# Padding rows written behind each expert's last row instead of a cleared row store, and another order of the first attention group

## What is computed

```python
x = x + attn(layernorm(x), w_qkv, w_proj, q_gain)
    # 16 query heads, 4 key/value heads of size 16, RMS norm and rotary embedding of q and k, causal softmax
x = x + ffn(layernorm(x), ...)
    # scores = sigmoid(x @ w_router); each token goes to its best 2 of 8 experts with normalised weights
    # expert: silu(x @ w1[e]) * (x @ w3[e]) @ w2[e], hidden width 176
    # plus a shared expert of hidden width 352 for all tokens
```

## Time and profile before

| | us |
|---|---|
| median of 3 runs | 584.66 (582.53 to 585.18) |
| profiled execution | 584.15 |
| its span | 582.2 |
| TensorE busy | 474.1 (81%) |
| ScalarE busy | 362.3 (62%) |
| VectorE busy | 313.5 (54%) |
| GpSimd busy | 170.9 (29%) |

### The profile page before, as it was taken

One profiled execution on the slowest core, in us unless ns is written; L12 is line 12 of the kernel. 1 busy time (PEld: TensorE's weight loads), 2 busy tenths in 40 slices (PEclk: granted clock), 3 DMA queues, 4 the chain that ended last, 5 costly groups with the idle time before them and its releaser, 6 DMA issues.

```text
span 582.2 us, 9830 instructions
## 1 busy us (share of the span) xinstructions
PE 474.1 (81%) x3202; PEld 264.9 (45%) x3202; DVE 313.5 (54%) x886; ACT 362.3 (62%) x567; POOL 170.9 (29%) x222
## 2 busy tenths in 40 slices
PE   1694869999999999999398768859797889999930
PEld 1582323233333333333143424327675789998920
DVE  6973516834713156131276555535957567666726
ACT  4255759989999989998369556615242335555520
POOL 3721101011110220103241172044455824444430
PEclk9878969999999999999599987868899989999985
DMA  8111012963999469243521022211011434444349
GB/s 207 31 48 41 11 32 86 301 163 98 289 296 282 112 48 4 1 92 98 145 55 57 2 74 86 62 43 56 28 57 40 124 74 119 124 117 125 110 138 340
DMA packets 77525, 61.36 MB, mean 105 GB/s; under 512 B 26984, under 2 KB 70600, under 8 KB 77480
## 3 DMA queue, kind: packets, MB, share of 16 engines
q1 hardware_dynamic: 73784, 51.04, 36.7%
q0 software_dynamic: 3408, 9.34, 4.5%
q10 hardware_dynamic: 288, 0.39, 0.2%
HBM read 19.88 MB, written 29.34 MB: 85 GB/s over the span
## 4 chain that ended last, share of the span: by engine, by line
PE 48%; DVE 18%; issue 14%; DMA 5%; POOL 5%; ACT 5%; SPq 4%; another core or an unknown queue 1%; DVEq 0%; ACTq 0%; POOLq 0%
PE ps L1575 16%; PE ps L1555 10%; PE ps L1747 6%; ACT prob L783 4%; PE ps L1765 3%; POOL rows_by_expert L658 2%; SPq L369 2%; PE ps L1584 2%; PE ps L1495 2%; DVE sm L922 2%; DMA yfin<-pair_out 2%; DVE sm L921 2%; PE ps L1769 1%; POOL hid_lo L687 1%; PE ps L1516 1%
## 5 line engine op out<-in xcount | busy, mean ns | idle before, releaser
L783 ACT ACTIVATE prob<-ps 128x1024 f32<-128x1024 f32 (+3 forms) x320 | 260.1, 919 | 70.6 <-PE ps L1555 68.6
L1575 PE MATMUL ps<-prob,v_sb 128*32 128x512 f32 (+3 forms) x1280 | 158.3, 569 | 18.3 <-DVE o_sb L1073 9.6
L1555 PE MATMUL ps<-qk 64*128 64x512 f32 (+3 forms) x640 | 121.1, 442 | 20.4 <-DMA qk<-qT 12.3
L617 POOL TENSOR_SCALAR_AFFINE_SELECT prob<-prob 128x512 f32<-128x512 f32 x64 | 41.3, 647 | 228.3 <-ACT prob L783 227.3
L1555 PEld LDWEIGHTS ps<-qk 64*128 64x128 f32 x640 | 54.1, 192 | 114.5 <-ACT prob L783 82.2
L1575 PEld LDWEIGHTS ps<-prob,v_sb 128*32 128x32 f32 x1280 | 26.0, 110 | 64.7 <-issue 34.0
L719 POOL DMA_INDIRECT pair_out<-yo,xg x39 | 37.5, 963 | 54.7 <-DVE yo L1431 54.4
L1073 DVE COPY o_sb<-ps 128x512 f32<-128x512 f32 x16 | 11.1, 691 | 65.2 <-PE ps L1575 64.6
L1693 PE MATMUL ps<-x2T,ws_hi 128*128 128x512 f32 (+1 forms) x96 | 33.0, 427 | 4.4 <-DVE hid L1300 4.4
L658 POOL DMA_INDIRECT rows_by_expert<-xs,slots x32 | 31.4, 981 | 14.2 <-issue 8.7
L1060 DVE CAST qT<-ps 96x512 fp32r<-96x512 f32 x16 | 11.0, 686 | 36.8 <-PE ps L1516 36.8
(11 more groups left out here) (203 smaller groups left out, 782.0 us busy)
## 6 DMA issues: line engine op xcount, KB each, us to landing
rows_by_expert<-pads SPq DMA_DIRECT2D x9, 1935.0 KB, 19.8
qk<-qT SPq DMA_DIRECT2D x138, 64.0 KB, 2.1
xg<-rows_by_expert SPq DMA_DIRECT2D x39, 129.0 KB
yfin<-pair_out SPq DMA_DIRECT2D x8, 512.0 KB, 7.3
stage<-in_w SPq DMA_DIRECT2D x8, 352.0 KB
x_sb<-in_x SPq DMA_DIRECT2D x4, 512.0 KB, 7.3
qk<-shT SPq DMA_DIRECT2D x8, 256.0 KB, 4.8
res<-in_x SPq DMA_DIRECT2D x4, 512.0 KB, 4.2
```

The source lines that it names most:

```text
L617: nc.gpsimd.affine_select(out=t, in_=t, compare_op=ALU.is_ge, fill=0.0, base=0, pattern=[[0, HPG], [1, P]], channel_multiplier=-1).then_in ...
L783: nc.scalar.activation(prob[:, u % NPB, 2 * hf:2 * hf + 2, c0:CH], ps[:, b:b + 2, c0:CH], ACT.Exp, scale=SCALE).then_inc(exp_done, 1)
L1555: ins = M(ps[:, 2 * (n % NSB) + h, c0:CH], qk[rows, par, PAIRS, kt * P:(kt + 1) * P], qk[rows, par, hf, j * CH + c0:(j + 1) * CH], start=T ...
L1575: ins = M(ps[VW * h:VW * (h + 1), O_BANK, c0:CH], v_sb[:, kt, :], prob[:, u % NPB, h, c0:CH], start=(kt == 0), stop=(u == LAST_OF[j]), ski ...
```

## The change

It does two things.

Rows: rows_by_expert is no longer filled. Each segment is T + 128 rows long (SEG). A new DRAM tensor `pad_rows` has 15 blocks of 128 padding rows (zeros with row numbers), one block to each of the 8 experts and to each of the 7 spare tiles. One DMA writes the zeros behind the moves of group 0, one the numbers behind those of group 1, and one copies the 7 spare blocks into place behind those of group 2. When the last `place` is done, VectorE casts `reach` to integers (`ends`). SyncE, behind its last weight load, waits for that and copies one block behind each expert's last row: 8 times a register load and a DMA from DRAM to DRAM. It then waits for all padding and all scattered rows before the gathers. `pair_out` shrinks. GpSimd's wait before the first scatter is removed.

First group: the round of chunk 1 stands ahead of `attend`, the round of chunk 2 at step 7 instead of 8, that of chunk 3 at step 14 instead of 16, and the output of chunk 0 at step 8 instead of 4. The scores of units 4 and 5, the first of chunk 1, are issued behind the value product of unit 3. VectorE's order follows.

```diff
-ROWS = E * T + SPARE * P
-PADS = 15
+SEG = T + P
+ROWS = E * SEG + SPARE * P
+PADS = E + SPARE
 FIRST_GROUP = {
-    0: [("round", 0, 1)], 4: [("out", 0, 0)], 8: [("round", 0, 2)], 12: [("out", 0, 1)], 16: [("round", 0, 3)],
+    7: [("round", 0, 2)], 8: [("out", 0, 0)], 12: [("out", 0, 1)], 14: [("round", 0, 3)],
...
+        pads_d = nc.dram_tensor("pad_rows", (PADS * P, ROW), F32, kind="Internal").ap()
+        pair_d = nc.dram_tensor("pair_out", (2 * T + PADS * P, D), F32, kind="Internal").ap()
...
             sp.wait_ge(consts, CONSTS)
-            clear_rows(0, 3)
+            sp.dma_start(pads_d.rearrange("(k p) c -> p k c", p=P), pads[:].broadcast_to([P, PADS, ROW])).then_inc(zeroed, 16)
             for c in range(NC):
                 move(1, c)
-            sp.wait_ge(s_ready, 2 * NU)
-            clear_rows(3, blocks)
+            sp.wait_ge(zeroed, 16)
+            sp.dma_start(pads_d[:, ID:ID + 1].rearrange("(k p) c -> p k c", p=P), pad_ids[:].bitcast(F32),
+                         allow_slow_non_contiguous=True).then_inc(padded, 16)
             for c in range(NC):
                 move(2, c)
-            sp.wait_ge(zeroed, 16 * blocks)
-            for b in range(blocks):
-                sp.dma_start(rows_d[b * PADS * P:(b + 1) * PADS * P, ID:ID + 1].rearrange("(k p) c -> p k c", p=P),
-                             pad_ids[:, b * PADS:(b + 1) * PADS, :].bitcast(F32),
-                             allow_slow_non_contiguous=True).then_inc(padded, 16)
+            sp.wait_ge(padded, 16)
+            sp.dma_start(rows_d[E * SEG:ROWS, :], pads_d[E * P:PADS * P, :]).then_inc(padded, 16)
             for c in range(NC):
                 move(3, c)
...
+            sp.wait_ge(ends_ready, 1)
+            for e in range(E):
+                end = nc.sync.value_load(ends[0:1, e:e + 1], min_val=e * SEG, max_val=e * SEG + T)
+                sp.dma_start(rows_d[bass.ds(end, P), :], pads_d[e * P:(e + 1) * P, :]).then_inc(padded, 16)
             sp.wait_ge(rows_ready, 1)
+            sp.wait_ge(padded, 16 * (2 + E))
             for j in range(NC):
                 sp.wait_ge(sent[j], 16 * 2 * TPC)
...
                 if part == 0:
-                    pool.wait_ge(padded, 16 * (ROWS // (PADS * P)))
                     pool.wait_ge(ids_ready, j + 1)
...
             scale_qk(0, TPC, 2 * TPC)
+            rotate(TPC, 2 * TPC)
             dve.wait_ge(qkv_ready, NT)
             values(0)
-            rotate(TPC, 2 * TPC)
+            take_round(0, 1)
             squares_qk(0, 2 * TPC, NT)
-            for c in range(1, NC):
-                take_round(0, c)
-                if c == 1:
-                    copy_output(0, 0)
-                    scale_qk(0, 2 * TPC, NT)
-                    take_output(0, 0)
-                if c == 2:
-                    output(0, 1)
-                if c < NC - 1:
-                    rotate(TPC * (c + 1), TPC * (c + 2))
+            copy_output(0, 0)
+            scale_qk(0, 2 * TPC, NT)
+            rotate(2 * TPC, 3 * TPC)
+            take_round(0, 2)
+            take_output(0, 0)
+            rotate(3 * TPC, NT)
+            output(0, 1)
+            take_round(0, 3)
...
+                V.tensor_copy(ends[:], reach[:]).then_inc(ends_ready, 1)
                 link(V.tensor_tensor(count, reach[:], bases[:], ALU.subtract))
...
                     u = q + LAG
-                    if u < NU:
+                    if isinstance(g, int) and g == 0 and TPC <= u < TPC + LAG:
+                        pass
+                    elif u < NU:
                         scores(g, u, (g + 1) % 2)
                     elif following:
                         scores(g + 1, u - NU, g % 2)
                     times_values(g, q)
                     exchange(g, schedule, q, parts_next)
+                    if isinstance(g, int) and g == 0 and q == TPC - 1:
+                        for u in range(TPC, TPC + LAG):
+                            scores(g, u, 1)
 
             for u in range(LAG):
                 scores(0, u, 1)
+            turn_round(1, 2)
             attend(0, FIRST_GROUP, True, NC + 1)
```

More of the change, by code:

```diff
@@ L98, in uses @@
     return sum(len(v) for v in schedule.values())
-X_FIRST = 1
+X_FIRST = 2
 X_MID = X_FIRST + uses(FIRST_GROUP)
@@ L106, in round_use @@
 def round_use(g, c):
-    if g == 0 and c == 0:
-        return 1
+    if g == 0 and c < X_FIRST:
+        return c + 1
     schedule, base = (FIRST_GROUP, X_FIRST) if g < 2 else (MID_GROUP, X_MID + (g - 2) * uses(MID_GROUP))
@@ L179, in build @@
         reach = sb("reach", [P, E], F32)
+        ends = sb("ends", [P, E], I32)
         tl = sb("tl", [P, 3, E], F32)
@@ L256, in build @@
         pads = sb("pads", [P, 1, ROW], F32, prep)
-        pad_ids = sb("pad_ids", [P, ROWS // P, 1], I32, prep)
+        pad_ids = sb("pad_ids", [P, PADS, 1], I32, prep)
         prep.close()
@@ L339, in build @@
         evicted = sem("evicted")
+        ends_ready = sem("ends_ready")
         rows_ready = sem("rows_ready")
@@ L359, in build @@
         rows_d = nc.dram_tensor("rows_by_expert", (ROWS, ROW), F32, kind="Internal").ap()
-        pair_d = nc.dram_tensor("pair_out", (2 * T + ROWS, D), F32, kind="Internal").ap()
+        pads_d = nc.dram_tensor("pad_rows", (PADS * P, ROW), F32, kind="Internal").ap()
+        pair_d = nc.dram_tensor("pair_out", (2 * T + PADS * P, D), F32, kind="Internal").ap()
         qk_f, qT_f, shT_f = (t[:].bitcast(F32) for t in (qk, qT, shT))
@@ L459, in move @@
                     move_shifts(g)
[L461 to L466, removed]
             sp.wait_ge(ones_ready, 2)
@@ L560, in _ @@
             numbered = 16
-            nc.gpsimd.iota(pad_ids[:, :, 0], pattern=[[P, ROWS // P]], base=2 * T, channel_multiplier=1).then_inc(consts, 1)
-            for to, n, step in ((levels[:], NT, P), (numbers[:], TILES, 1), (bases[:], E, T)):
+            nc.gpsimd.iota(pad_ids[:, :, 0], pattern=[[P, PADS]], base=2 * T, channel_multiplier=1).then_inc(consts, 1)
+            for to, n, step in ((levels[:], NT, P), (numbers[:], TILES, 1), (bases[:], E, SEG)):
                 nc.gpsimd.iota(ints[:, 0:n], pattern=[[step, n]], base=0, channel_multiplier=0).then_inc(consts, 1)
@@ L1278, in list_tiles @@
                 prefix = wide[:, 0:E * E].rearrange("p (e f) -> p e f", f=E)
-                V.tensor_scalar(back, tiles, -float(P), float(T), ALU.mult, ALU.add)
+                V.tensor_scalar(back, tiles, -float(P), float(SEG), ALU.mult, ALU.add)
                 link(V.tensor_tensor(prefix, upto[:], tiles.unsqueeze(1).broadcast_to([P, E, E]), ALU.mult))
```

## The result

The changed kernel takes 588.4 us (median of 7 runs, 587.68 to 591.0) beside 584.66 us before (median of 7, 582.53 to 585.58): ratio 1.0086, 95% interval 1.0059 to 1.0113. A second comparison on another chip gave 1.0101 (1.0057 to 1.0145). It is slower by about 0.9%; the forecast was 589.1. The profiled execution has a span of 585.9 us, 3.7 more than before.

A forecast was written before the change was run, and what follows sets the result against it. It took three limits: exponentials in groups 1 and 2, moves into qk in the first group, SyncE's gathers at the expert tiles' start. 584.15 + 0 - 4.3 + 9.2 = 589.05 us; 8-in-10 range 584.3 to 593.0.

The forecast's parts named there:

- Part 1: Groups 1 and 2 of attention: removing the row-store clearing gains 0 us, as no queue behind those writes is late.
- Rival 3: Groups 1 and 2: removed traffic was holding something, so the clearing gives 2.8 us, total 586.3; chance 0.10.
- Part 2: First attention group: the new order shortens TensorE's waits for moves into qk, gaining 4.3 us, range 3.3 to 5.3.
- step (b): First group, chunk 2: transposes one unit ahead start 3.9 us earlier, scores at 73.9 us; gain 3.9 us.
- Step (a): First group, chunk 1: transposes start 2.5 us earlier, scores start at 54.0 us; gain 2.35 us.
- Rival 2: First group gives nothing back because another wait replaces the removed one; 593.4 us, chance 0.10.
- Part 3: Start of expert tiles: SyncE's eight padding copies delay the first tile, with clock loss 9.2 us, range 7.5 to 10.6.
- The clock term: Start of expert tiles: after idling, TensorE runs at half speed for 4 to 6 us, costing 1.7 us.
- Rival 1: SyncE at 462 us: copies issue faster; overlapped loads delay tile 0 only 2.3 us, total 582.2; chance 0.15.
- Rival 4: Start of expert tiles: padding copies hide behind the scattered rows, total 579.9 us; chance 0.02.

The follow-up runs named there:

- order alone: Kernel before with only the first group's new order, row store still cleared: 0.992 of the kernel before, 0.9897 when repeated.
- rows alone: Changed kernel with the first group's old order put back, so only the rows change remains: 1.0143 of the kernel before.
- register loads first: Changed kernel with SyncE's eight register loads all done before the eight padding copies: 1.0106 of the kernel before.
- the two lots: Changed kernel with four padding copies ahead of each of SyncE's last two weight loads: 1.0006 of the kernel before.

## Why the prediction was right

**Part 1 (0 us): right.** Column B is 138.0 to 138.1 us in the three profiles with the old order and 137.8 in all with the new one, whether the store is cleared or not. Rival 3 is dead.

**Part 2 (4.3 us): right in size by the timed runs** (4.6 us by 0.992, 6.0 by 0.9897), and step by step in one profile of eleven (53.72 for 54.0, 73.68 for 73.9); in the other ten chunk 2's scores gained 1.1 to 2.7 us, not 3.9. What it lacked is that step (b), "that distance doesn't shrink, because ScalarE paces it", holds only at full clock. At 0.50 TensorE paces it, and the distance from the restart to chunk 2's transposes grew from the 11.2 us of the prediction to 68.39 - 55.75 = 12.6 (10.9 in the order alone). Column A is 81.2 to 83.7 us in the eleven profiles with the new order and 84.5 to 87.0 in the three with the old one, so the gain there is real, but mostly below 3 us against the kernel before, and the column moves by 2 us without the change too. The timed gain thus isn't all found in group 0. In the two profiles of the order alone columns B and D give 0.2 to 0.6 us more, and column F is 0.7 to 1.0 shorter than in the kernel before, which the prediction had nothing for; the agreement of 4.3 with 4.6 is in part luck.

Step (a) has a slip that cancelled. Issues from 51.12 on that take 2.02 us end at 53.14, and a landing of 2 us behind that gives 55.1, not 54.0. But the step also took it that ScalarE's keys would hardly leave earlier than before. In the order alone they left at 50.01, 1.0 us earlier counted from the first scores; the last issue ended at 51.78, and the scores started 1.9 us later. In the changed kernel's profile they left at 52.34, as the products ahead of unit 3's scores ran at half clock. Rival 2 didn't come to pass in the timed runs, though something like it, the clock, took more than half of the gain of chunk 2's scores in four profiles and part of it in six more.

**Part 3 (9.2 us): right in sum, by errors that cancel.** The delay of the first tile was forecast as 7.5; column D gives 7.75, 8.7 and, for the rows alone, 7.5. Its terms: the first copy 1.5 us behind SyncE's last load, not 1.1; 1.29 us a copy, not 1.11 (its own issue takes 0.50 us where the gather's takes 0.34, and the step between load and issue is longer); landing 2.40, not 2.6; 0.8 to the gather's issue, not 1.1; and 2.1 us from there to TensorE, not 3.2, for in the earlier trace rows TensorE came to the rows behind its other work, when they must have landed: 2.1 us is a gather's landing in the order alone too, where TensorE came 0.8 us after it. That last term was mis-sized most: I read the end of other work as the landing. The clock term was 1.7. The half clock came as forecast, up to about 478.7 us, 5.6 us behind the restart at 473.07, but column E is only 0.3 and 0.8 us longer (changed less before in each pair), and E itself moves by 1.3 us between the two profiles of the kernel before. Missing from the sum was column F, 0.6 to 1.3 us. The last copy of 129 KB had landed 2.40 us after its issue, the other seven 2.4 to 3.2. With the Trainium skill (DMA: Bandwidth & Descriptors, Anatomy of one DMA), whose fit gave an estimated 2.3 us, the trace agrees.

**The other rivals.** Rival 1's overlap doesn't exist (register loads first, above). Its "2.3 us late, too short to lose the clock" has nothing in the runs to rest on: in the order alone TensorE stood still for only 1.74 us before 53.72, though with shorter pauses around it, and was granted 0.57 and 0.58 in the windows at 56 to 58 and 58 to 60 us. Rival 4, hiding all copies behind the scattered rows, can't be had behind the last load, as argued; with the copies moved ahead the first tile comes within 1.6 us of its due.

**Sum.** 589.05 was built on the profiled execution; the measured ratios 1.0086 and 1.0101 are 5.0 and 5.9 us on 584.66, the forecast's net 4.9. The span's own difference, 3.7, isn't a better measure: column C happened to be 3.3 us shorter in that profile, and its first scores stood 0.94 later. The sum hides errors of its parts: by the timed runs the order gave 4.6 to 6.0 us and the rows cost 8.3 for the forecast 4.3 and 9.2, and within the 9.2 the clock was put too high and the last loads were left out.

## What to carry to other kernels

Here, work taken from a queue that nobody waited for was worth nothing, however many bytes it moved; work added behind the last free moment of a queue counted in full, and eight register-addressed DMAs cost eight times load plus issue, 1.3 us each, even though each moves only 129 KB. Before such a change ask when the queue is idle early enough, and what stands behind the place to which it is moved. And compare stretches over several profiles before crediting a change with a difference of a few us: here up to 7 us came and went in a stretch whose code never changed.

## What the runs showed of the hardware

TensorE's clock was granted at half (1.2 GHz) at 50 to 52 us of the changed kernel, although TensorE was busy in all of that window; the kernel before had the full clock at the same place. What before it decides this was not tried. Behind the wait of 8.78 us at the tiles it was granted half at 476 to 478 us too; the kernel before, with no such wait, had the full clock 2 to 4 us behind its first tile.

One stretch of group 3, with the same code in every kernel, took 49.0 to 56.3 us, and 50.5 and 56.2 in two executions of the same kernel, with a wait of ScalarE for up to 4.3 us, in which TensorE's semaphore increment came up to 3.1 us behind the recorded end of its instruction.

The same loads from DRAM, 4 MB in all, ran at 342 GB/s instead of 378 when 3.0 MB of unused rows were allocated ahead of their tensor.

A register-addressed DMA of 128 rows on SyncE came every 1.11 us where DRAM is its source and SBUF its target, and every 1.29 us from DRAM to DRAM behind the last weight load (1.36 with all eight ahead of the last two loads, 1.76 and 1.48 in the two lots); with the register loads taken out it was 0.70 us.
